# A decoder layer on one core: the first u product of blocks 0 to 4 stands one step sooner in TensorE's order

## What is computed

```python
xr = x @ W_in.T                                   # 512 -> 2 x 1024
xc, res = (xr[..., :DI], xr[..., DI:])
u = silu(conv(xc, 4 taps, causal, per channel) + b_conv)
x_dbl = einsum('bdl,ed->ble', u, W_xproj)         # dt (32), B (16), C (16)
delta = softplus(dt @ W_dt.T + b_dt)
h = exp(delta * A) * h + delta * B * u            # a scan over 512 times, 16 states
y = (sum over states of h * C + u * D) * silu(res)
return y @ W_out.T
```

## Time and profile before

| | us |
|---|---|
| median of 3 runs | 2486.76 |
| lowest, highest of the 3 | 2473.32, 2489.14 |
| the profiled execution | 2481.5 |
| its span in the profile | 2479.7 |
| mean granted TensorE clock in it | 0.983 of full speed |

### The profile page before, as it was taken

One profiled execution on the slowest core, in us unless ns is written; L12 is line 12 of the kernel. 1 busy time (PEld: TensorE's weight loads), 2 busy tenths in 40 slices (PEclk: granted clock), 3 DMA queues, 4 the chain that ended last, 5 costly groups with the idle time before them and its releaser, 6 DMA issues. The chain is left out here.

```text
span 2479.7 us, 38405 instructions
## 1 busy us (share of the span) xinstructions
PE 2328.2 (94%) x15232; PEld 1387.1 (56%) x15232; DVE 1837.8 (74%) x2164; ACT 1564.3 (63%) x2604; POOL 1675.1 (68%) x911
## 2 busy tenths in 40 slices
PE   8888999999999999999999998997799999999998
PEld 4565666566565666556666655564445554554543
DVE  4998898898899899889889887772465466366463
ACT  4786787878778788778787887751433443333332
POOL 1898899898899889889989988882333233143130
PEclk9999999999999999999999999999899999999999
DMA  6677878887877888787887787876000110000000
GB/s 206 140 154 162 217 158 177 219 171 163 211 161 172 186 196 178 157 223 162 177 218 171 165 219 154 192 159 211 28 28 7 35 35 1 34 18 1 18 17 17
DMA packets 103525, 329.57 MB, mean 133 GB/s; under 512 B 9571, under 2 KB 46819, under 8 KB 72627
## 3 DMA queue, kind: packets, MB, share of 16 engines
q0 software_dynamic: 27648, 201.34, 41.3%
q1 hardware_dynamic: 75699, 125.78, 14.9%
HBM read 107.25 MB, written 18.51 MB: 51 GB/s over the span
## 5 line engine op out<-in xcount | busy, mean ns | idle before, releaser
L1020 POOL TENSOR_TENSOR mamba_ring<-mamba_ring,mamba_c_row 128x1024 f32<-128x1024 f32 x512 | 1277.7, 2652 | 45.2 <-DVE mamba_ring L908 44.3
L908 DVE TENSOR_TENSOR_SCAN mamba_ring<-mamba_ring,ps 128x512 f32<-128x512 f32 x1024 | 1175.1, 1201 | 142.6 <-PE ps L452 136.9
L713 ACT ACTIVATE mamba_ring<-mamba_delta,mamba_a_neg 128x512 f32<-128x512 f32 x1024 | 659.7, 710 | 79.0 <-DMA mamba_ring<-mamba_ring 77.7
L452 PEld LDWEIGHTS ps<-shared,mamba_v_t 64*128 64x128 f32 x8192 | 499.4, 189 | 249.3 <-issue 149.7
L452 PE MATMUL ps<-shared,mamba_v_t 64*128 64x128 f32 x8192 | 581.1, 284 | 53.8 <-DVE mamba_ring L908 52.8
L1029 POOL DMA_DIRECT2D mamba_ring<-mamba_ring x192 | 181.0, 943 | 147.2 <-DMA mamba_ring<-mamba_ring 117.2
L1674 POOL TENSOR_TENSOR xf_pr<-xf_pr,xf_top 128x1232 f32<-128x1232 f32 x32 | 75.0, 2343 | 256.6 <-DVE xf_top L1577 256.6
L418 PE MATMUL ps<-mamba_xt,mamba_wres 128*128 128x512 f32 x512 | 242.4, 617 | 0.0
L361 PE MATMUL ps<-mamba_xt,mamba_wu 128*128 128x512 f32 x464 | 218.5, 615 | 5.6 <-DMA mamba_xt<-x_t 5.6
L882 DVE SCALAR_TENSOR_TENSOR mamba_u<-ps,mamba_wcv,mamba_u 128x511 f32<-128x511 f32 (+2 forms) x192 | 142.1, 740 | 73.5 <-ACT mamba_u L678 71.0
L504 PE MATMUL ps<-mamba_wout,mamba_u 128*128 128x512 f32 x352 | 168.0, 611 | 0.0
(11 more groups left out here) (149 smaller groups left out, 2842.4 us busy)
## 6 DMA issues: line engine op xcount, KB each, us to landing
mamba_ring<-mamba_ring POOLq DMA_DIRECT2D x192, 1024.0 KB, 7.8
mamba_c_row<-c_rows SPq DMA_DIRECT2D x32, 1024.0 KB, 11.4
mamba_wres<-w_res SPq DMA_DIRECT2D x64, 256.0 KB, 6.1
mamba_wu<-w_u SPq DMA_DIRECT2D x58, 256.0 KB, 4.1
x_rows<-x SPq DMA_DIRECT2D x32, 256.0 KB, 9.0
mamba_xt<-x_t SPq DMA_DIRECT2D x7, 1024.0 KB, 10.6
x<-x_rows SPq DMA_DIRECT2D x28, 256.0 KB, 5.0
xf_xn<-x SPq DMA_DIRECT2D x16, 256.0 KB, 7.9
```

The source lines that it names most:

```text
L452: m = nc.tensor.matmul(ps[:, 2 * s + i, tb * P:(tb + 1) * P], v_t[g % 2][i * H:(i + 1) * H, tb * P:(tb + 1) * P], diag_b[i * H:(i + 1) * H ...
L713: a = nc.scalar.activation(ring[:, q % NR, i, :], delta[:, d % EARLY, :], ACT.Exp, scale=a_neg[:, d, 2 * k + i:2 * k + i + 1])
L908: m = nc.vector.tensor_tensor_scan(ring[:, r, i, :], ring[:, r, i, :], both[:, bass.ds(i, T, 2)], 0.0, ALU.mult, ALU.add)
L1020: nc.gpsimd.tensor_tensor(ring[:, q % NR], ring[:, q % NR], c_row[:, 2 * k:2 * k + 2, :], ALU.mult).then_inc(c_done, 1)
```

## The change

```diff
                 if feeds and d < 5:
                     n = (b + 1) * ND + FIRST_U[d]
-                    if k == 1:
+                    if k == 0:
                         u_product(n, BANK_A, range(KT))
                     if k == 5 and d in TWO_U:
```

## The result

| | before | changed |
|---|---|---|
| median us | 2478.88 (19 runs) | 2488.68 (19 runs) |
| lowest, highest | 2466.6, 2489.14 | 2483.73, 2495.74 |
| profiled execution, its span | 2481.5, 2479.7 | 2492.17, 2490.4 |

What follows compares the result with a forecast made beforehand. VectorE waits for a late TensorE, for B products (136.9 us) and first taps (71.0 us). Blocks 0 to 4 cost +23, shorter diagonal stalls return 8: +15, giving 2496.5 or 2501.8, said as 2499 us, range 2484 to 2516.

Steps and rivals of the forecast that it cites:

- d=0: Block 0: the last output product and step 2's B products come late, delaying the tap; +0.9 us a pass.
- d=1: Block 1: the moved product fills TensorE's 1.23 us idle, step 2's scan ends later; +0.2 us a pass.
- d=2: Block 2: neither engine idles there, so step 2's B products and scan come late; +1.2 us a pass.
- d=3: Block 3: the output product and step 2's B products come late, delaying add, scan and tap; +1.5 us a pass.
- d=4: Block 4: TensorE idled 1.06 us there, and the second product can start 0.1 us sooner; -0.1 us a pass.
- What may take it back: Block 7's long VectorE diagonals: pass 4's probably goes (-4), pass 0's absorbs 1, pass 2's half the time (-3); -8 us.
- The +19: Block 7: sum if a diagonal waits for one GpSimd instruction only, with 8 us and not 17 to give back.
- (d): Faster: step 2's B products in time in blocks 0 to 4, 25 us of idle goes; 2460 us, chance 0.07.
- (b): No stall goes, new ones come in other passes, or x_t lands late: +23 to +40, about 2515 us; chance 0.22.
- (c): Nothing measurable: all three stalls of block 7 vanish, -17 against +23, about 2490 us; chance 0.13.
- x_t: Transfer for the next pass, needed 12.6 us after issue, median landing 10.6; counted as nothing, at worst 15 us.
- (a): As worked block by block: +8 to +24 us, 2489 to 2511 us; chance 0.58.

Runs made afterwards that it cites:

- e1 to e4: Kernel before, first u product moved to step 0 only in block 0, block 2, block 3, or blocks 1 and 4: 0.999, 1.000, 1.0007, 0.9985.
- e9: Kernel before, with both of VectorE's diagonals for the next pass made by GpSimd instead: 1.0012, median 2480.92 us.
- e3_d3: Kernel before, with only block 3's first u product moved to step 0: 1.0007 (0.9997 to 1.0017).
- e8_taps_later: Kernel before, u product left in step 1, VectorE's three taps of the first product one step later: 1.0008 (0.9991 to 1.0025).
- e11_best: e9 with the first u product moved to step 0 in block 4 alone and taps a step later in blocks 0, 1, 3: 1.0012, median 2480.37 us.

## Why the prediction was right

**Block by block.** Worked out and measured, a pass: d=0 +0.9, measured 0.8 to 1.0; d=1 +0.2, 0.1; d=2 +1.2, 1.1; d=3 +1.5, 1.2 at full clock and 2.4 in the four passes where it dropped; d=4 -0.1, -0.2 to -0.1. Pass 0 was given +1 and had +0.6 in block 0 but -1.5 in block 1, where the first product before fell into a stretch at the half clock level and had its tap wait 3.2 us. e1 to e4 show the same for each block by itself. The trace method held because the orders are fixed: one pass, followed instruction by instruction, stands for six. That the sum of +23 met the measured +24.6 so closely is part luck: 4.8 of the 24.6 are clock drops and 1.8 a block 0 behind a quick block 7, neither of which was in the sum, and pass 0 gave 1.3 back where 1 was to be lost.

**What may take it back.** Size -8, measured -11.4 in block 7. The diagonals' own excess fell by 8.6 us, which is the size; the rest is what stands behind a long diagonal, above all TensorE at half clock, a term that the prediction did not have. The 8 also met by luck, for the passes were wrong: pass 4's, on which half of it was put, stayed at 4.4 us, pass 2's went whole (-6.1, of which half was counted), and pass 0's became shorter, 5.4 for 7.5 us. The +19 that a wait for one GpSimd instruction would give is not borne out: the stalls ran over up to four. The reason given was half of it. I had the diagonal as the price and GpSimd's lag as its occasion; e9 shows that the lag costs time without any diagonal too. Of the 4.3 us between +15 and the +10.7 of the profiled spans, 1.8 are in these two sums and 2.5 in the other columns, mainly the part behind the Mamba pass, which the change does not touch.

**The rivals.** (d), faster, needed B(d, 2) in time. In blocks 0, 1, 2 and 4 of passes 1 to 6 the scan waited 0.4 to 1.2 us for it; in block 3 it found it ready, which I had named a sign of being wrong, but only because the late add had held VectorE longer, as the working for d = 3 has it. (b) needed no stall to go. (c), all of it given back, was wrong by half. x_t, for which I took nothing, cost nearly nothing: its median landing was later (14.1 for 10.6 us), past the 12.6 us that I had called well inside, yet behind the start TensorE waited for it only in pass 3, for 0.5 us, and in the others its weight loads for 0.3 us or less.

**The expected signs** came nearly all as written: the taps' idle fell by more than the 20 us I had put (32), the scans' rose by 31; the adds of (0, 1) and (3, 1) wait about 2 us each; pass 3 took 204.11 us for 197.82, of which 1.2 are the clock's and 1.8 a block 0 behind a quick block 7; I had said 3 to 4. There were two long diagonals instead of three. The blind point was the level: 19 runs put the kernel before at 2478.9, 8 us below the median of the three that I had. The 2499 that I said is 10 us above the measured 2488.7, half of it the level from which I counted and half the size, +15 for +9.8. So 2488.7 lies just under the 2489 to 2511 of (a), my own case, though +9.8 is inside its +8 to +24.

## What to carry to other kernels

When two engines are both nearly full and strictly ordered, an idle time in front of one consumer is not slack: moving its producer ahead makes whatever the producer jumps over late, and the wait only changes its line (32 us of taps' idle became 31 us of scans' idle in the changed kernel, and 35 became 34 in e8_taps_later). Look for what stands between the old place and the new one, above all things that another engine waits for in the next step; here putting the output product back ahead gave back 0.5 us of the 1.2 that block 3 lost at full clock, and nothing in block 0, where the B products behind it were as late. And before pricing a stall by the instruction that shows it, ask which engine is behind: here a third, lagging one gave back about half of the loss in the profiled executions, and took back the gain of e11_best.

## What the runs showed of the hardware

A VectorE multiplication of two SBUF tensors, 0.67 us by itself, took up to 8.0 us (e8_taps_later) when it was issued during GpSimd multiplications. It did not get in between one GpSimd multiplication and the next: behind the start of the kernel there are 33 that took over 1 us, in eleven kernels, and each ended 0.56 us behind the end of a GpSimd multiplication which was followed by a DMA issue and not by another multiplication. With the same multiplication on GpSimd it took 1.33 us each and nothing waited for it.

TensorE's clock went to its half level behind an idle of 2.02 us in four passes of the changed kernel, and not behind the same idle in two others or in five of six passes of e3_d3; the loss was 1.2 us each time. It also went there in or behind the idle of 3.7 to 6.5 us that each of the three long diagonals of the kernel before gave TensorE. What decides it at 2 us these runs don't show.
